# A pre-norm layer with a gated scan and a top-2 expert layer on one core: fewer routing operations on VectorE, router logits made by expert in four column groups of the array, and two small GpSimd operations placed ahead of queued scatters

## The reference, cut to what matters

```python
x = x + scan_layer(layernorm(x), w_qkva, gamma)      # x: 8 groups x 1024 tokens x 256
x = x + expert_layer(layernorm(x), router_w, w0, w1, wo)

# expert_layer, 8 groups of 1024 tokens, 8 experts, C = 256 places for each expert and group
raw   = softmax(x @ router_w)                         # 1024 x 8
idx1  = argmax(raw);  gate1 = raw[idx1]               # mask m1 = one_hot(idx1)
rest  = raw * (1 - m1)
idx2  = argmax(rest); gate2 = rest[idx2]              # mask m2 = one_hot(idx2)
p1    = cumsum(m1) - m1;                 m1 = m1 * (p1 < C)
p2    = cumsum(m2) - m2 + count(m1);     m2 = m2 * (p2 < C)   # count over the kept firsts
dispatch each token to place p1 of idx1 and place p2 of idx2
hidden = gelu(tokens @ w0) * (tokens @ w1)            # 256 -> 1368 -> 256, for each expert
out    = gate1 * y(idx1, p1) + gate2 * y(idx2, p2)    # a token that has no place gets 0
```

## Time and profile before

| | |
|---|---|
| median of 3 runs | 1660.02 us (1657.38 to 1660.55) |
| the profiled execution, its own time | 1646.57 us |
| its span, first to last instruction | 1644.8 us |
| PE busy | 1615.6 us, 98% |
| DVE busy | 939.4 us, 57% |
| ACT busy | 762.1 us, 46% |
| POOL busy | 506.2 us, 31% |
| mean granted TensorE clock | 0.997 |

### The profile page before, as it was taken

The page is one execution under the profiler, slowest core; times in us unless marked ns, Lnnn a source line. Parts: engine busy times, 40 slices in busy tenths (PEclk is TensorE's granted clock), DMA queues, the critical chain, the costliest instruction groups (busy, mean ns, idle before and its releaser), DMA issues.

```text
span 1644.8 us, 22948 instructions
## 1 busy us (share of the span) xinstructions
PE 1615.6 (98%) x8450; PEld 1393.2 (85%) x8450; DVE 939.4 (57%) x1955; ACT 762.1 (46%) x1389; POOL 506.2 (31%) x433
## 2 busy tenths in 40 slices
PE   7999998999999999999999999999999999999998
PEld 6888887888888888888888888888888888888887
DVE  7999844446544564456444754465445644464442
ACT  5777634335443443445333543354434433453343
POOL 2166666651222222222222222222222222222111
PEclk9999999999999999999999999999999999999999
DMA  7554121036222442234222611152224422342211
GB/s 170 161 161 124 54 80 54 4 59 141 47 40 39 91 90 38 36 82 92 38 33 35 140 34 36 36 130 51 39 39 88 93 36 38 76 97 34 33 14 14
DMA packets 193848, 110.94 MB, mean 67 GB/s; under 512 B 96008, under 2 KB 189640, under 8 KB 193736
## 3 DMA queue, kind: packets, MB, share of 16 engines
q1 hardware_dynamic: 165064, 75.37, 18.3%
q0 software_dynamic: 28672, 34.10, 12.9%
HBM read 60.11 MB, written 34.61 MB: 58 GB/s over the span
## 4 chain that ended last, share of the span: by engine, by line
PE 73%; SPq 7%; POOL 5%; DVE 5%; DMA 5%; issue 4%; ACT 2%; POOLq 0%; ACTq 0%; DVEq 0%
PE bank L1692 21%; PE bank L1715 19%; PE bank L1731 14%; PE bank L1733 7%; PE bank L1504 5%; SPq L509 3%; POOL out L727 3%; SPq L426 2%; POOL slots L658 2%; DMA out<-xring,slot_records 2%; DMA stage<-in_L_ffn_wo_kernel 1%; PE bank L1706 1%; PE bank L1557 1%; DVE y L1441 1%; SPq L427 1%
## 5 line engine op out<-in xcount | busy, mean ns | idle before, releaser
L727 POOL DMA_INDIRECT out<-xring,slot_records x128 | 215.4, 1683 | 859.3 <-DVE xring L1411 794.1
L923 ACT ACTIVATE hhi<-y 128x512 fp32r<-128x512 f32 (+1 forms) x349 | 220.4, 631 | 514.1 <-DVE y L1441 463.5
L1731 PE MATMUL bank<-wo,hhi 128*128 128x512 f32 (+1 forms) x1276 | 443.9, 385 | 3.3 <-DVE hlo L1444 3.1
L1441 DVE TENSOR_TENSOR y<-bank,sig 128x512 f32<-128x512 f32 x320 | 220.7, 690 | 323.3 <-PE bank L1715 314.3
L1733 PE MATMUL bank<-wo,hlo 128*128 128x256 f32 x1396 | 382.8, 274 | 0.0
L1444 DVE TENSOR_TENSOR hlo<-y,hhi 128x512 fp32r<-128x512 f32 (+1 forms) x349 | 241.7, 693 | 243.5 <-ACT hhi L923 243.5
L1731 PEld LDWEIGHTS bank<-wo,hhi 128*128 128x128 f32 (+1 forms) x1276 | 239.1, 187 | 52.2 <-DVE hlo L1444 5.7
L913 ACT ACTIVATE sig<-bank 128x512 f32<-128x512 f32 x320 | 189.5, 592 | 198.9 <-PE bank L1692 198.2
L1733 PEld LDWEIGHTS bank<-wo,hlo 128*128 128x128 f32 x1396 | 262.1, 188 | 8.4
L1692 PE MATMUL bank<-xThi,whi 128*128 128x512 f32 (+1 forms) x704 | 216.1, 388 | 1.7 <-ACT sig L913 1.2
L1692 PE MATMUL bank<-xTlo,whi 128*128 128x512 f32 (+1 forms) x704 | 212.3, 382 | 0.0
(11 more groups left out here) (147 smaller groups left out, 1726.7 us busy)
## 6 DMA issues: line engine op xcount, KB each, us to landing
stage<-in_L_ffn_w_kernel SPq DMA_DIRECT2D x160, 128.0 KB, 3.2
rows<-rows SPq DMA_DIRECT2D x448, 32.0 KB, 1.9
stage<-in_L_ffn_wo_kernel SPq DMA_DIRECT2D x80, 128.0 KB, 3.3
xring<-in_L_attn_x SPq DMA_DIRECT2D x16, 512.0 KB, 4.8
out<-xring SPq DMA_DIRECT2D x16, 512.0 KB, 4.2
x_rows<-rows SPq DMA_DIRECT2D x16, 512.0 KB, 3.2
slots<-records,sloti POOLq DMA_INDIRECT x128, 2.1
rows<-x_rows,slot_records POOLq DMA_INDIRECT x128, 2.9
```

Source lines behind the costliest of these rows:

```text
L727: pool.indirect_dma_start(out_rows, bass.IndirectOffsetOnAxis(idx, 0), ysb[:, t % 2, j, :], None, compute_op=ALU.add).then_inc(added, 16)
L923: act.activation(h_high(e, t, hc)[0:n, :], hf[0:n, hc % 2, :], ACT.Copy).then_inc(h_hi, 1)
L1441: dve.tensor_tensor(hf[0:n, hc % 2, :], up_value(e, t, hc)[0:n, :], gel[0:n, hc % 2, :], ALU.mult).then_inc(mul_done, 1)
L1731: pe.matmul(lines(yb[j][:, :]), high, lines(wo[0:n, hc, :, :].rearrange("p s c -> p (s c)")), start=hc == 0, stop=end, skip_group_check=True)
```

## The change

Records are 4 numbers instead of 8, and each of a token's two places gets a record of its own with its own gate in it. So `gates` and its DVE operations go away, and ACT and DVE scale by the record's gate directly. `choose` writes the gates into the records itself, and the wait that keeps a record from being overwritten before its scatter has landed moves from `place` to `choose`. `place` has 6 operations instead of 12: `count` now adds the number of first choices to the sums of the second choices on PE (8 more small matmuls for a group), one product covers both masks, and a dropped token's place is moved up by the number of places. The sums count all first choices and not only the kept ones.

`route` makes the logits by expert: the router's 8 columns, padded to 32, are the stationary side and 128 tokens the moving side, and the four tiles of a half group write to four groups of 32 partitions. ACT copies the result to SBUF (`copy_logits`), and one transpose (`route_back`) turns it back, so that there is one more ACT copy and one more PE transpose for each half group. In the steps the transpose of half 1 stands one `third` (a projection of six matmuls) after its `route`; that of half 0 stands after `third(i, 1, 1, "kv")` and `transpose2`. In the drain, `choose(g, 0, 2)` moves from chunk 0 to chunk 1 of its tile. On POOL, `powers2` of group 7 half 0 moves ahead of n = 36 to 39 and of the wait for the rows of `gather(0, 1)`, and that of half 1 moves ahead of n = 40 to 42.

```diff
-    REC = 8
+    REC = 4
@@ scatter, on POOL
                             slots[:, :], bass.IndirectOffsetOnAxis(sloti[:, g.ring(RING), k, t:t + 1], 0),
-                            records[:, g.ring(RING), t, :], None).then_inc(scattered[t // HT][g.parity], 16)
+                            records[:, g.ring(RING), k, t, :], None).then_inc(scattered[t // HT][g.parity], 16)
@@ after the steps, on POOL
             gather(0, 1)
+            powers2(last_group, 0)
             pool.wait_ge(rows_loaded[1], 16 * FJ)
             scatter(left, left + 4)
-            powers2(last_group, 0)
-            scatter(left + 4, late - 5)
             powers2(last_group, 1)
-            scatter(late - 5, late)
+            scatter(left + 4, late)
@@ on ACT
-                wait(act, logits, g, 2, h)
+                wait(act, logits_t, g, 2, h)
+            def copy_logits(g, h):
+                wait(act, logits_t, g, 2, h + 1)
+                act.activation(by_expert, lgT, ACT.Copy).then_inc(logits_copied, 1)
@@ step, on ACT
                 if Dg:
+                    copy_logits(i.plus(-2), 1)
                     exponent(i.plus(-2))
...
                     sigmoid(i, 1, 1)
+                if C and B:
+                    copy_logits(i.plus(-1), 0)
@@ choice, on DVE
                 elif n in (5, 11):
-                    dve.reduce_max(gate[:, k, :], p[:, :, :], AXX).then_inc(choose_chain, 1)
+                    if n == 5:
+                        for h in range(2):
+                            wait_scattered(dve, g, h)
+                    dve.reduce_max(gate, p[:, :, :], AXX).then_inc(choose_chain, 1)
@@ placing, on DVE: the six operations after
+                    dve.tensor_tensor(pos[:, :, :, :], cum, mask[:, :, :, :], ALU.mult).then_inc(cum_read, 1)
                     dve.reduce_sum(psel[:, :, :].rearrange("p k t -> p (k t)"),
                                    pos[:, :, :, :].rearrange("p k t e -> p (k t) e"), AXX).then_inc(place_chain, 1)
+                    dve.tensor_scalar(dropped[:, :, :], psel[:, :, :], float(CAP), float(NSLOT), ALU.is_ge, ALU.mult)
                     dve.scalar_tensor_tensor(out=slotf[:, :, :], in0=top[:, :, :], scalar=-float(ESLOTS),
                                              in1=psel[:, :, :], op0=ALU.mult, op1=ALU.add).then_inc(place_chain, 1)
+                    dve.scalar_tensor_tensor(out=sloti[:, g.ring(RING)].rearrange("p k t -> p (k t)"),
                                              in0=slotf[:, :, :].rearrange("p k t -> p (k t)"),
                                              scalar=float(E * ESLOTS + g.value * CAP),
+                                             in1=dropped[:, :, :].rearrange("p k t -> p (k t)"),
+                                             op0=ALU.add, op1=ALU.add)
+                    dve.tensor_scalar(records[:, g.ring(RING), :, :, TOK].bitcast(I32),
+                                      tokid[:, :].unsqueeze(1).to_broadcast([P, 2, TILES]), float(g.value * S), None,
                                       ALU.add).then_inc(routed, 1)
@@ step and experts, on DVE: gates(e, t) and the count of expert_no are gone
-                    gates(0, 0)
                     prepare(0, 0, 0)
...
                 dve.wait_ge(rows_free, FT * e + t + 1)
+                dve.wait_ge(records_loaded[t], 16 * (e + 1))
...
-                                             scalar=gslot[:, t % 2, j:j + 1], in1=part[:, j, :],
+                                             scalar=slot_records[:, t, j, GATE:GATE + 1], in1=part[:, j, :],
@@ route and count, on PE
-                for j in range(HT):
-                    for k in range(KD):
-                        at = (h * HT + j) * E
-                        last = pe.matmul(lg[:, at:at + E], x2nT[:, k, j * P:(j + 1) * P], router[:, k, :],
-                                         start=k == 0, stop=k == KD - 1)
-                last.then_inc(logits, 1)
+                for k in range(KD):
+                    for j in range(HT):
+                        last = pe.matmul(lgT[j * QUAD:(j + 1) * QUAD, :], router[:, k, :],
+                                         x2nT[:, k, j * P:(j + 1) * P], start=k == 0, stop=k == KD - 1)
+                last.then_inc(logits_t, 1)
+
+            def route_back(g, h):
+                wait(pe, logits_copied, g, 2, h + 1)
+                at = h * HT * QUAD
+                pe.transpose(lg[:, at:at + LOGIT_ROWS], by_expert[0:LOGIT_ROWS, :],
+                             ident[0:LOGIT_ROWS, 0:LOGIT_ROWS]).then_inc(logits, 1)
...
-                    rest = TILES - t
-                    last = pe.matmul(cum[:, :, t + 1:TILES + 1, :], ones[:, :],
-                                     mask[:, :, t:t + 1, :].to_broadcast([P, 2, rest, E]),
+                    rest = TILES - t - 1
+                    if rest:
+                        pe.matmul(cum[:, :, t + 1:TILES, :], ones[:, :],
+                                  mask[:, :, t:t + 1, :].to_broadcast([P, 2, rest, E]), start=False, stop=False)
+                    last = pe.matmul(cum[:, 1, :, :], ones[:, :], mask[:, 0, t:t + 1, :].to_broadcast([P, TILES, E]),
                                      start=False, stop=t == TILES - 1)
```

More of the change, by code:

```diff
@@ L108, in build @@
     PW = D // NB
-    GT1, GT2, EX1, TOK, SRC = range(5)
+    GATE, TOK, SRC = range(3)
     ESLOTS = G * CAP
@@ L212, in build @@
         hf = y[:, 0]
+        by_expert = part[:, 0, 0:P]
+        LOGIT_ROWS = (HT - 1) * QUAD + E
         value_low, value = y[0:HF, 1, 0, :], y[0:HF, 1, 1, :]
@@ L603, in _ @@
             pool.memset(ones[:, :], 1.0)
-            pool.memset(records[:, :, :, :], 0.0).then_inc(consts_raw, 1)
+            pool.memset(records[:, :, :, :, :], 0.0).then_inc(consts_raw, 1)
             pool.memset(zero[:, :], 0.0)
@@ L608, in _ @@
             pool.iota(fill[:, :, :, SRC].bitcast(I32), pattern=[[0, 2], [0, FJ]], base=2 * S, channel_multiplier=0)
-            for r in range(0, RING, 2):
-                pool.iota(records[:, r:r + 2, :, SRC].bitcast(I32), pattern=[[S, 2], [P, TILES]], base=0,
+            for r in range(RING):
+                pool.iota(records[:, r, :, :, SRC].bitcast(I32), pattern=[[0, 2], [P, TILES]], base=S * (r % 2),
                           channel_multiplier=1)
@@ L1079, in choice @@
                 k, p = (0, raw) if n < 10 else (1, ex)
+                gate = records[:, g.ring(RING), k, :, GATE]
                 if n == 0:
@@ L1137, in placing @@
                     wait(dve, cum_read, g, 1, 1)
-                    dve.tensor_tensor(pos[:, 1, :, :], pos[:, 1, :, :], second_mask, ALU.mult).then_inc(place_chain, 1)
-                elif n == 4:
-                    wait(dve, place_chain, g, 7, 2)
                     dve.reduce_sum(psel[:, :, :].rearrange("p k t -> p (k t)"),
                                    pos[:, :, :, :].rearrange("p k t e -> p (k t) e"), AXX).then_inc(place_chain, 1)
-                elif n == 5:
-                    wait(dve, place_chain, g, 7, 3)
-                    for h in range(2):
-                        wait_scattered(dve, g, h)
-                    dve.scalar_tensor_tensor(out=row_gates, in0=psel[:, :, :], scalar=float(CAP), in1=gate[:, :, :],
-                                             op0=ALU.is_lt, op1=ALU.mult).then_inc(place_chain, 1)
-                elif n == 6:
+                elif n == 2:
+                    wait(dve, place_chain, g, 2, 1)
+                    dve.tensor_scalar(dropped[:, :, :], psel[:, :, :], float(CAP), float(NSLOT), ALU.is_ge, ALU.mult)
+                elif n == 3:
@@ L1150, in placing @@
                     dve.scalar_tensor_tensor(out=slotf[:, :, :], in0=top[:, :, :], scalar=-float(ESLOTS),
                                              in1=psel[:, :, :], op0=ALU.mult, op1=ALU.add).then_inc(place_chain, 1)
[L1152 to L1154 removed]
+                elif n == 4:
+                    wait(dve, place_chain, g, 2, 2)
+                    dve.scalar_tensor_tensor(out=sloti[:, g.ring(RING)].rearrange("p k t -> p (k t)"),
@@ L1314, in step @@
                 if Dg:
-                    place(back2, 0, 4)
+                    place(back2, 0, 1)
                 outputs(i, 1, 0)
@@ L1321, in step @@
                 if Dg:
-                    place(back2, 4, 5)
+                    place(back2, 1, 2)
                 if A:
@@ L1325, in step @@
                 if Dg:
-                    place(back2, 5, 7)
+                    place(back2, 2, 4)
                 if A:
@@ L1336, in step @@
                 if Dg:
-                    place(back2, 8, 9)
+                    place(back2, 4, 5)
                 if S:
@@ L1340, in step @@
                 if Dg:
-                    place(back2, 9, 12)
+                    place(back2, 5, 6)
                 if S:
@@ L1391, in drain @@
                 if (t, hc) == (0, 9):
-                    place(before_last, 0, 4)
+                    place(before_last, 0, 1)
                 if (t, hc) == (0, 10):
-                    place(before_last, 4, 12)
```

(9 more changed lines are left out.)

107 lines of the change are left out of this document (39 added, 68 removed).

## The result

| | before | after |
|---|---|---|
| median | 1660.55 us (1657.38 to 1661.47, 5 runs) | 1690.24 us (1688.61 to 1690.67, 5 runs) |
| ratio | | 1.0175, 95% interval 1.0163 to 1.0188 |
| span of the profiled execution | 1644.8 us | 1688.6 us |
| PE busy | 1615.6 us | 1613.7 us |
| mean granted TensorE clock | 0.997 | 0.988 |

Ratios are of fast executions alone; the one slow execution of all that follow is in e7 (2762.85 us, at a granted clock of 0.557).

A forecast was written before the change was run, and what follows sets the result against it. PE and DVE bound the steps, then POOL's scatter backlog. PE's 4.2 + 7.2 + 1.2 = 12.6 us was capped at 6.2 + 2.5 = 8.7, less 0.7 for the clock: 8.0 us, 1652.0 us, range 1646 to 1659.

The forecast's parts named there:

- part 4: After the steps, powers2 ahead of scatters: PE loses 7.2 us of stalls, but POOL's backlog limits the result to 8.0.
- rival (b): PE isn't held at the rows of gather(0, 3): nearly the whole 12.6 us counts, 1647.4 us; chance 0.13.
- Part 1: Route on PE: 1.70 to 0.9 us, transpose back 0.15, count +0.3; 1.0 us off PE a step.
- (c): Column groups don't overlap, route stays at 1.70 us: 2.5 to 3 us gained, 1657.3 us; chance 0.17.
- (d): Route dearer than before, slower measurably above 2.3 us each; at 3.5 us 15 us slower, 1675; chance 0.05.
- Part 2: DVE in the steps: fewer place operations save 0.6 us a step; the wait moved into choose costs nothing.
- Part 3: What holds the steps' gains back (POOL, SP, transfers): everything 4.2 us earlier at 188.12 us.
- (a): POOL's chain of scatters binds: 8.0 us gained, range 5 to 11, 1652.0 us; chance 0.57.
- (e): Late variance for powers2 of half 1, or late logits, undo gains: 0 to 2 us gained, 1659; chance 0.08.

The follow-up runs named there:

- e7: e1 with the kernel before's order of powers2 of group 7 on POOL, behind scatters; 1658.32 us, ratio 0.9980 to before.
- e1: Changed kernel with records of 8 numbers (32 bytes) instead of 4 (16 bytes); 1655.29 us, ratio 0.9951 to before.
- e2: Changed kernel with 16-byte records written to places 32 bytes apart; 1661.76 us, ratio 1.0004 to before.
- e10: Changed kernel, 16-byte records 16 bytes apart, places of a tile's two groups interleaved; 1659.25 us, ratio 1.0006 to before.
- e8: Changed kernel with 32-byte records written 64 bytes apart; 1654.67 us, ratio 0.9963 to before.
- e3: e1 with the old route (tokens stationary, no copy or transpose back, choose in chunk 0); 1662.43 us, ratio 1.0006 to before.
- e5: Kernel before again without an edit, for a second profile; 1663.06 us, one run.
- e4: Kernel before with only the changed kernel's order of powers2 of group 7 on POOL; 1662.49 us, ratio 0.9997 to before.

## Why the prediction was wrong

**The step that failed** is in part 4 and rival (b): "the pace of pairs is 4 issues and a wait, not bytes". From this I priced the halved record at nothing, and even gave it a chance of a gain. The pace is 4 issues and a wait, but the wait is for the landing, and this depends on the writes. It went from 1.4 us a pair to 2.8 to 3.7 us, with single ones of 7.87 us. I had bounded every PE and DVE operation that the trace didn't show, and not the transfer, though a 16-byte indirect write stood in no row of before. The cause is shown from three sides: e1 (size back), e2 (distance back) and e10 (neighbours written in different groups).

The Trainium skill has a rule that points at this: DMA: Bandwidth & Descriptors, Specifications, gives 512 bytes as the smallest transfer for full rate, and says that the engine does a read, a modification and a write below it. That two such writes in one place disturb each other would fit. But e1 and e8 write 32 bytes, far below this size, and show no such loss, so the rule's bound isn't the one that decided here.

**Part 1** was right in kind and too careful in size. Route: 0.58 us for the 0.9 that I took, a little above the lower bound of 0.45; transpose back 0.03 for 0.15; `count` 0.18 more, for the 0.3. Off PE per half group are thus 1.70 - 0.58 - 0.03 = 1.09 us, less the 0.1 named below. Rivals (c) and (d) are refuted. The drain at a change of tiling that TensorEngine Tiling, Key Properties, in the Trainium skill speaks of costs little at most: from the last records of the projection to the route it is 0.54 us (130.03 to 130.57) instead of the 0.44 between others (129.59 to 130.03), so 0.1 us on this side, and on the other it is within the 0.58.

**Part 2** saved on DVE what it should and more (in step 3 the six operations of `place` are busy 1.3 us in e3, the twelve 2.2 us in e5; I took 0.6 off), but it decides nothing by itself: e3, which has it with the old route, is at 1.0006. The moved wait cost nothing in e1; no DVE row there waits for scatters.

**Part 3** held once the record is taken out: 4.2 us earlier on POOL forecast for the batch behind 188.12, and e1 starts its counterpart at 193.08 where e5 has 197.82, 4.7 us. Part of this is the shorter stall of ACT (3.34 us for 6.69). Ahead of the stall PE's last transposes of `rows` start at 179.56 us in e1, 182.26 in e3 and 183.59 in e5: 4.0 us earlier, 2.7 of it the route's. Of the late logits there is a trace as I feared: DVE waits 4.6 us in four waits for them in e1, which this gain includes. In the changed kernel itself the small slack of `powers2` (0.28 us) turned round: it handed POOL's delay to DVE and PE, 6 us in step 4.

**Part 4.** The stalls of the earlier trace rows went as forecast, and the gain with them only in part: nothing in e4, 2 to 5 us in e7 against e1, not 7.2 before POOL's limit. POOL's backlog binds, as (a) has it, but not where I looked. In e1 PE waits 3.33 us for the rows of `gather(0, 1)` (about 3 forecast), 2.38 us for those of `gather(0, 2)`, and not at all for those of `gather(0, 3)` at 348.84 us, where I had expected 4; by my own list that is a sign against (a). And in e4, where PE was early enough, the first weights of expert 1 stopped it at 400 us. I had put no term for them, though they wait for the same backlog. Of (e) there is a bit: `powers2` of half 1 stands 1.80 us for the variance in e1. I had also read the end of the stalls off a profile without the idle times that e5 and all others have near 185 us.

In rival (d) "5 us more than in (c)" should be 3, with which its 2.3 us and its 1675 are worked out; its chance doesn't change.

**The sum without the record.** With 32-byte records the ratio is 0.9951, which makes 0.9951 x 1660.02 = 1651.9 us, against the forecast 1652.0; by the medians, 0.9965, it makes 1654.2. So close an agreement is partly luck: part 1 gave more than I took, part 4 less, and PE was held at other places than in my sum.

## What to carry to other kernels

A smaller record is an edit of its own: price the landing of an indirect write and not only its issue, and look which neighbours are written close together in time. Where an engine waits for transfers to land, every operation queued behind that wait inherits a change in the landing; the slack of the smallest of them (0.28 us for `powers2`) tells how soon it spreads. When a backlog ends earlier, look for everything that stands behind it and not only for the first: here the rows of a gather had 2.5 us of slack by my estimate, and the next expert's weights about 1 by e4. Take the slack and the stalls from two profiles before adding them up, as one execution can lack a stall of 3 to 7 us that the others have.

## What the runs showed of the hardware that I had not expected

- Indirect writes of 16 bytes to neighbouring places, made by the same group's scatters, land late: POOL's gap for a pair is 2.8 to 3.7 us late in the backlog, against 1.4 us with 32 bytes. With 16-byte writes whose neighbours aren't written then it is 1.4 to 2.2 us, whether they lie 32 or 16 bytes apart. With 32 bytes it makes no difference whether they are 32 or 64 apart (1.4 us).
- Matmuls with 32 stationary columns in four column groups overlap: 16 records of 128 moving f32 columns take 0.58 us, 0.036 each, where f32 transposes of the whole array pace at 0.10.
- A landing wait after every eight transfers instead of every four made the kernel 1.5% slower than before with 11.5 us of landing waits instead of 40.1.
